# A gated two-block decoder on one core: quantisation groups padded by their minimum, inputs loaded in halves, work redistributed among the engines

## Time and profile before

| what | value |
|---|---|
| median of 3 runs | 260.58 us (259.67 to 260.72) |
| the profiled execution | 258.16 us, its span 256.4 us |
| busy shares | PE 86%, DVE 64%, ACT 53%, POOL 44% |
| mean granted clock of TensorE | 0.960 |

### The profile page before, as it was taken

The page is one execution under the profiler, slowest core; times in us unless marked ns, Lnnn a source line. Parts: engine busy times, 40 slices in busy tenths (PEclk is TensorE's granted clock), DMA queues, the critical chain, the costliest instruction groups (busy, mean ns, idle before and its releaser), DMA issues. The chain is left out here.

```text
span 256.4 us, 5210 instructions
## 1 busy us (share of the span) xinstructions
PE 221.2 (86%) x1960; PEld 179.7 (70%) x1960; DVE 165.0 (64%) x430; ACT 135.9 (53%) x286; POOL 111.6 (44%) x163
## 2 busy tenths in 40 slices
PE   8489988591999898985889999997998999999992
PEld 8366656470867676765767787776886788888882
DVE  1777886799289999885536667778746433353333
ACT  2144875974276786767876677764354222222230
POOL 3211111167166667656193777778947600000000
PEclk9869999978699999998999999999999999999999
DMA  4999001750000000000000000000000000020002
GB/s 138 382 359 364 21 1 18 309 165 0 3 0 1 0 3 0 1 0 4 0 3 3 3 3 4 3 3 3 4 1 0 0 3 0 0 84 0 0 0 82
DMA packets 9288, 12.59 MB, mean 49 GB/s; under 512 B 1072, under 2 KB 7984, under 8 KB 9264
## 3 DMA queue, kind: packets, MB, share of 16 engines
q1 hardware_dynamic: 8832, 12.07, 13.4%
q10 hardware_dynamic: 432, 0.20, 0.3%
HBM read 11.22 MB, written 1.05 MB: 48 GB/s over the span
## 5 line engine op out<-in xcount | busy, mean ns | idle before, releaser
L1416 PE MATMUL PB<-SGN,WHI 128*128 128x512 f32 x128 | 40.5, 398 | 0.0
L768 DVE TENSOR_TENSOR QM<-SIL,PB 128x512 f32<-128x512 f32 x16 | 11.0, 688 | 31.7 <-ACT SIL L1102 31.7
L1219 PE MATMUL PB<-SGN,XQH 128*128 128x512 f32 x64 | 27.3, 426 | 2.5 <-DVE XQL L619 2.5
L315 POOL TENSOR_TENSOR RSTD<-MVS,MHALF 128x1 f32<-128x1 f32 x24 | 14.5, 603 | 32.4 <-DVE MVS L473 32.4
L1102 ACT ACTIVATE SIL<-PB 128x512 f32<-128x512 f32 x16 | 9.6, 599 | 34.8 <-PE PB L1416 34.8
L1433 PE MATMUL PB<-WHI,SGN 128*128 128x256 f32 x128 | 25.8, 284 | 1.4 <-DVE SGN L776 1.4
L1219 PE MATMUL PB<-SGN,XQL 128*128 128x512 f32 x64 | 26.6, 415 | 0.0
L1416 PEld LDWEIGHTS PB<-SGN,WHI 128*128 128x128 f32 x128 | 23.1, 188 | 4.2
L1416 PE MATMUL PB<-SGN,WLO 128*128 128x512 f32 x64 | 25.2, 394 | 0.0
L356 POOL TENSOR_TENSOR HBQ<-HBQ,HSD 128x512 f32<-128x512 f32 x16 | 16.7, 1046 | 17.6 <-ACT HBQ L1008 17.6
L1058 ACT ACTIVATE HBQ<-PB 128x512 f32<-128x512 f32 x32 | 17.5, 614 | 10.8 <-PE PB L1356 10.8
(11 more groups left out here) (138 smaller groups left out, 553.9 us busy)
## 6 DMA issues: line engine op xcount, KB each, us to landing
WRAW<-w_dram SPq DMA_DIRECT2D x3, 1024.0 KB, 9.5
...
CTX<-ctx_dram SPq DMA_DIRECT2D x1, 1024.0 KB, 11.5
...
```

The source lines that it names most:

```text
L315: nc.gpsimd.tensor_tensor(RSTD[:, bass.ds(t, 1)], MVS[:, bass.ds(t, 1), 1], MHALF[:], ALU.pow).then_inc(rstd_ready, 1)
L768: nc.vector.tensor_tensor(GU[:, b, :], SG[:, b, :], PB[2 * b + 1][:], ALU.mult).then_inc(d_g, 1)
L1219: mm = nc.tensor.matmul(PB[2 * half + m][:], part[:, p, c, :], sgn(m, c, a, b), start=(c == 0 and k == 0), stop=(c == DC - 1 and k == 1))
L1416: mm = nc.tensor.matmul(PB[2 * b + m][:], wcol(w_part, m, c, j), act_part[:, c, g * TG:(g + 1) * TG], start=(c == 0 and i == 0), stop=(c = ...
```

## The change

Several edits are made together.

- **Padded groups.** XN (normalised x) and HB (h) get 65 columns per group of 64; the 65th holds 1e-5, written once by GpSimd. The maximum over 65 columns is then already max(|x|, 1e-5), and the instruction that formed the step (lines 584 and 657) goes. The factor 127 moves: for x into a small GpSimd product (`x_factor`), for h into the scale of ScalarE's first rounding instruction, and 1/127 into the weights' scales WSC.
- **x for the quantised layer.** ScalarE normalises it (`norm_x`) from an offset that GpSimd prepares (`x_offset`). For the first two tiles GpSimd takes over scaling and multiplying back. The rounding (`x_round`) reads XV as 5 rows of 64 out of 65 and writes 320 columns to XW. The tiles of the first attention are still normalised by VectorE.
- **Loads in halves.** x, CTXT and CTX are loaded as first halves, then second halves; the small vectors but one go behind the weights.
- **k and v.** The eight parts go to step numbers 1 to 7 (two in step 2), k through bank 4 to ScalarE, v through bank 5 to VectorE. VectorE sums |w1| and |w2| in eight slices of 512; ScalarE writes the signs of w3 in stage A too. The product that sums the scales moves from behind the first `gate_up` to the last step of stage A, and the setup of stage C's vectors (`prepare_c`) from ahead of VectorE's step 0 of stage B to its steps 3 to 5.
- **Order.** `down_scale` moves from the end of VectorE's step 1 up behind its first product. ScalarE rounds the second half of the previous tile before its other work. `xt_c` of the first tile moves into the last step of stage B, `q` behind it, and ScalarE loads the exponential's table ahead of the last rounding.

The core of the diff:

```diff
 WARMUPS = 14
-KV_PARTS = (("k", 0), ("k", 1), ("v", 0), ("k", 2), ("v", 1), ("k", 3), ("v", 2), ("v", 3))
-KV_AT = (1, 2, 3, 4, 5, 6, 7, 8)
+KV_PARTS = (("k", 0), ("v", 0), ("k", 1), ("k", 2), ("v", 1), ("k", 3), ("v", 2), ("v", 3))
+KV_AT = (1, 2, 2, 3, 4, 5, 6, 7)
+SIGN_ORDER = (0, 2, 4, 6, 1, 3, 5, 7)
+SIGN_AT = {3: (0, 1, 2), 4: (3, 4), 5: (5, 6), 6: (7, 8), 7: (9, 10, 11)}
+ABS_AT = {3: (0, 1), 4: (2, 3), 5: (4,), 6: (5, 6), 7: (7,)}
...
+        XN = sb("XN", [P, 2, D // GS, GS + 1])
         XSD = sb("XSD", [P, 2, 4])
...
-        XV = sb("XV", [P, D])
+        XRS = sb("XRS", [P, 4])
+        XV = sb("XV", [P, D // GS + 1, GS + 1])
+        XW = sb("XW", [P, D + GS])
...
+        HB = sb("HB", [P, 2, FF // GS, GS + 1])
...
+            for half, names in enumerate((("x", "ctxt", "ctx"), ("x2", "ctxt2", "ctx2"))):
+                ts = slice(half * NT // 2, (half + 1) * NT // 2)
+                ns = slice(half * NT // 2 * P, (half + 1) * NT // 2 * P)
...
-                             ).then_inc(ld[part], 16)
-            sp.dma_start(CTXT[:], ctx_t.rearrange("c p n -> p c n")).then_inc(ld["ctxt"], 16)
-            sp.dma_start(CTX[:], ctx.rearrange("t p d -> p t d")).then_inc(ld["ctx"], 16)
+                             ).then_inc(ld[names[0]], 16)
+                sp.dma_start(CTXT[:, :, ns], ctx_t.rearrange("c p n -> p c n")[:, :, ns]
+                             ).then_inc(ld[names[1]], 16)
+                sp.dma_start(CTX[:, ts, :], ctx.rearrange("t p d -> p t d")[:, ts, :]
...
+            sp.dma_start(BK[:], bk).then_inc(ld["bk"], 16)
...
+            def x_offset(t):
+
+                nc.gpsimd.tensor_tensor(NMB[:, t:t + 1], MVS[:, t, 0:1], NEG1[:], ALU.mult
+                                        ).then_inc(nm_x, 1)
+                pool.wait_ge(nm_x, 2 * t + 1)
+                pool.wait_ge(rstd_ready, t + 3)
+                nc.gpsimd.tensor_tensor(NMB[:, t:t + 1], NMB[:, t:t + 1], RSTD[:, t:t + 1],
+                                        ALU.mult).then_inc(nm_x, 1)
...
+            def x_factor(t):
+                pool.wait_ge(b_xd, 5 * t + 2)
+                nc.gpsimd.tensor_tensor(XRS[:], XR[:], C127[:].broadcast_to([P, D // GS]),
+                                        ALU.mult).then_inc(b_xd, 1)
+
+            def x_scale(t, p):
+                x_factor(t)
+                pool.wait_ge(b_xd, 5 * t + 3)
+                nc.gpsimd.tensor_tensor(XV[:, 0:D // GS, 0:GS], XN[:, p, :, 0:GS],
+                                        XRS[:].unsqueeze(2).broadcast_to(x_groups), ALU.mult
+                                        ).then_inc(b_xd, 1)
+
+            def x_quantised(t, p):
+                pool.wait_ge(b_xd, 5 * t + 5)
+                pool.wait_ge(xt_done, NT + t - 1)
+                nc.gpsimd.tensor_tensor(x_view(XQ[:, p, :]), x_view(XW[:, 0:D]),
+                                        XSD[:, p, :].unsqueeze(2).broadcast_to(x_groups),
+                                        ALU.mult).then_inc(b_xq, 1)
+
+            def step_a(t, p):
+                if t in (6, 7):
+                    x_quantised(t - 6, t - 6)
+                if t in (5, 6):
+                    x_scale(t - 5, t - 5)
+                if live(t - 2):
+                    rstd(t - 2, t - 2)
+                    x_offset(t - 2)
...
-                if half == 0:
-                    norm(0, 0, 0)
-                    norm(1, 1, 0)
-                    dve.wait_ge(ld["mask"], 16)
-                    nc.vector.tensor_scalar(MASKB, MASK8[:], -1.0, NEG, ALU.add, ALU.mult
-                                            ).then_inc(set_dve, 1)
-
...
+            stats_half(0)
+            dve.wait_ge(ld["mask"], 16)
+            nc.vector.tensor_scalar(MASKB, MASK8[:], -1.0, NEG, ALU.add, ALU.mult
+                                    ).then_inc(set_dve, 1)
+            norm(0, 0, 0)
+            norm(1, 1, 0)
...
-                    valid_gate()
+                    stats_half(1)
+                    gate_rows()
...
-                for k in {3: (0, 1), 4: (2, 3), 5: (4, 5), 6: (6,), 7: (7,)}.get(t, ()):
-                    nc.vector.tensor_reduce(ABSP[:, k:k + 1], WRAW[:, 0, k * D:(k + 1) * D],
+                if t == 5:
+                    dve.wait_ge(ld["w0b"], 16)
+                for k in ABS_AT.get(t, ()):
+                    nc.vector.tensor_reduce(ABSP[:, k:k + 1], flat(WRAW)[:, k * 512:(k + 1) * 512],
                                             AX.X, ALU.add, apply_absolute_value=True
                                             ).then_inc(w_abs1, 1)
-
...
+                if t in (5, 6):
+                    x_round(t - 5)
+                if t in (4, 5):
+                    x_absmax(t - 4, t - 4)
+                    x_recip(t - 4)
+                if t == NT - 1:
+                    dve.wait_ge(w_abs1, NT)
+                    nc.vector.tensor_reduce(ABSS[:, 0:2],
+                                            ABSP[:, 0:NT].rearrange("p (m k) -> p m k", m=2), AX.X,
+                                            ALU.add).then_inc(wsum, 1)
+                    lo_x(0, 0)
+                    dve.wait_ge(wsum, 2)
+                    nc.vector.tensor_scalar(WSC[:, 0:2], PB[2][:, 0:2], 1.0 / (D * FF * QB), None,
+                                            ALU.mult).then_inc(wsc, 1)
+
...
+                dve.wait_ge(xn_done, t + 1)
                 need(dve, b_xq, t - 1)
-                nc.vector.tensor_reduce(XSD[:, p, :], x_view(XH[:, p, :]), AX.X, ALU.max,
+                nc.vector.tensor_reduce(XSD[:, p, :], XN[:, p, :, :], AX.X, ALU.max,
                                         apply_absolute_value=True).then_inc(b_xd, 1)
 
-            def x_step(t, p):
+            def x_recip(t):
                 dve.wait_ge(b_xd, 5 * t + 1)
-                nc.vector.tensor_scalar(XSD[:, p, :], XSD[:, p, :], Q_EPS, 1.0 / QB, ALU.max,
-                                        ALU.mult).then_inc(b_xd, 1)
...
-                    norm(u, p, 1)
                     x_absmax(u, p)
-                    x_step(u, p)
-                    x_recip(u, p)
+                    x_recip(u)
                 h_product(t, p, 0)
+                if t == 1:
+                    down_scale()
+                h_absmax(t, p, 0)
+                h_recip(t, p, 0)
                 if live(t - 1):
                     lo_h(t - 1, 0)
-                h_absmax(t, p, 0)
-                h_step(t, p, 0)
-                h_recip(t, p, 0)
                 if live(t - 2):
                     update_b(t - 2, p)
                 if live(t + 1):
                     lo_x(t + 1, 1 - p)
                 if live(u):
-                    x_round(u, p)
+                    x_round(u)
...
-                h_step(t, p, 1)
                 h_recip(t, p, 1)
                 if live(t - 1):
                     lo_h(t - 1, 1)
...
-                if t == 1:
-                    down_scale()
-
...
+            def norm_x(t, p):
+
+                act.wait_ge(nm_x, 2 * t + 2)
+                need(act, b_xd, 5 * (t - 2) + 4)
+                nc.scalar.activation(XN[:, p, :, 0:GS],
+                                     X[:, t, :].rearrange("p (g s) -> p g s", s=GS), ACT.Identity,
+                                     bias=NMB[:, t:t + 1], scale=RSTD[:, t:t + 1]
+                                     ).then_inc(xn_done, 1)
...
+                if t == 6:
+                    act.wait_ge(ld["w3"], 16)
+                if 3 <= t <= 5:
+                    norm_x(t - 3, (t - 3) % 2)
+                for k in SIGN_AT.get(t, ()):
+                    sign_slice(k)
...
+                nc.scalar.activation(h, h, ACT.Copy, bias=MAGIC, scale=QB).then_inc(b_w, 1)
...
+                if live(t - 1):
+                    round_h(t - 1, 1 - p, 1)
                     hi_h(t - 1, 0)
                 if live(t + 1):
                     hi_x(t + 1, 1 - p)
-                if live(t - 1):
-                    round_h(t - 1, 1 - p, 1)
+                else:
+                    copy_ht(0, 0, 4, xt_done, c_q, c_ht, 2 * NT)
                 silu(t, 1)
...
+                if live(t + 3):
+                    norm_x(t + 3, 1 - p)
+                if 2 <= t <= 6:
                     hi_slice(t - 2)
-
-            warm(ACT.Silu)
-            sign_w3(0)
-            act.wait_ge(ld["bias"], 16 * 8)
-            act.wait_ge(a_mk, NT)
-            act.wait_ge(wsc, 1)
-            pipeline(step_b, lag=0)
-            copy_ht(0, 0, 4, xt_done, c_q, c_ht, 2 * NT)
-            round_h(NT - 1, 1, 1)
-            hi_h(NT - 1, 0)
-            q_out(0)
-            hi_h(NT - 1, 1)
-
...
+            warm(ACT.Silu)
+            act.wait_ge(a_mk, NT)
+            act.wait_ge(wsc, 1)
+            pipeline(step_b, lag=0)
+            q_out(0)
             warm(ACT.Exp)
-            copy_ht(1, 1, 4, xt_done, c_q, c_ht, 2 * NT)
+            round_h(NT - 1, 1, 1)
+            hi_h(NT - 1, 0)
             for b in range(4):
                 exp_c(0, 0, b)
+            hi_h(NT - 1, 1)
```

(19 more changed lines are left out.)

438 lines of the change are left out of this document (199 added, 239 removed).

## The result

The changed kernel takes 243.63 us (median of 4 runs, 242.29 to 245.47), the kernel before beside it 260.65 (259.67 to 261.41): a ratio of 0.935, 95% interval 0.928 to 0.942. The forecast was 244.7, 239.5 to 251.

The account below looks back on a forecast made before the run. TensorE nearly fills stage A's loop; VectorE, held by GpSimd, lengthens stage B's steady steps; TensorE waits at B's start and end. Terms -2.0 - 7.1 - 4.8 - 2.0 = -15.9 give 242.3 profiled, 244.7 beside the median; range 239.5 to 251.

Parts of the forecast that it names:

- (a): Begin and stage A, up to the first gate_up: halved loads start the loop earlier; -2.0 us, between -3.4 and 0.
- rival 3: Stage A: VectorE bounds it, sums and evictions bunching in the middle steps; 2.0 us back, 246.7; chance 0.06.
- TensorE's 27.30 are unchanged: Loop of stage A: TensorE's busy time stays 27.30 us, so the loop itself has little to give.
- (b): First two steps of stage B, 21.74 us: they shrink to the later steps' length; -7.1 us, bounds -7.7 and -3.4.
- Rival 2: Start of stage B: the low clock remains, a new wait replacing the removed one; 3.7 us back, 248.4; chance 0.09.
- (c): Five steady steps of stage B, 41.31 us: VectorE no longer bounds; -4.8 us, bounds -6.1 and 0.
- my 7.3: Steady steps of stage B: forecast 7.3 us per step, TensorE's work at full clock, 7.55 x 0.97.
- longer than VectorE's 7.09: Steady steps of stage B before: 8.26 us each, longer than VectorE's busy 7.09, taken as 35.43 / 5.
- Rival 1: Steady steps of stage B stay at 8.26 us, GpSimd's queue full; 4.8 us back, 249.5; chance 0.13.
- (d): End of stage B, 19.19 us: wait of 3.31 goes, less the table load's 1.28; -2.0 us, bounds -3.3 and 0.
- The rest: Stages C and D, to the last product: they keep their instructions; 0 us change.
- Rival 4: All of stage B at the low clock from small recurring waits; slower, 25 us above the forecast, 269.5; chance 0.06.

Follow-up runs that it names:

- a_combined: Changed kernel with stage C's setup behind VectorE's step 7, ScalarE's exponentials last at stage B's end, and 24 instead of 14 products of ones: 242.62 us.
- a_whole_loads: Changed kernel with x loaded in its two halves first, then CTXT and CTX whole, as before: 245.38 us.
- b_scale_early: Kernel before, with only the instruction for the scale of w3 moved up behind the first product of VectorE's step 1: 257.11 us, ratio 0.989.
- a_setup_late: Changed kernel with five of eight setup instructions of stage C moved from VectorE's steps 3 to 5 of stage B to behind step 7: 243.62 us.
- a_load_late: Changed kernel with ScalarE's load of the exponential's table behind the last rounding instead of ahead of it: 246.43 us.
- a_tail: Changed kernel with ScalarE's list at the end of stage B reordered, the four exponentials of tile 0 last: 244.32 us.

## Why the prediction was right, point by point

**(a) Right in the mechanism, half the size.** From x to the loop's first scores it is 8.13 us before (13.87 - 5.74) and about 6.2 after (both tiles' scores stand in one row, begun at 10.60), 1.9 sooner, where I had 2.1. Then 1.3 of it went again, so that 0.64 are left; the other 0.31 of the 0.95 are x, which landed sooner. It did not go to VectorE as rival 3 had it (26.50 busy of 32.54; I had 26.5) but to the half clock, which in the kernel before ended at 17.16 and now at 19.11, and of which the loop, starting sooner, meets more. The step that failed is "TensorE's 27.30 are unchanged". From the second tile's scores on, where the loop of the earlier trace rows starts too, after and then a_combined have:

```profile
11.61:43.14 31.53, 29.35 (x117) 19.84 (x117) 26.41 (x98) 19.27 (x51) 9.33 (x25) 0.88 0.50 172
```

```profile
11.83:42.01 30.18, 26.26 (x118) 17.74 (x117) 26.31 (x98) 19.16 (x51) 9.33 (x25) 1.00 0.50 173
```

TensorE's work is 29.35 at a clock of 0.88, and 26.26 at 1.00. Which of halves and other edits of stage A gave what is left stays open: a_whole_loads is within the spread.

GpSimd's power took 1.32 beside the mask in its new place, against 1.03: 0.29 of the 0.69 us that I had as the limit. The Trainium skill, "SBUF — State Buffer", section "Who interferes with whom", by which the one that issues first holds the shared ports and the other blocks, had led me to weigh this. The row that I had called in agreement shows less than that: there the power of 1.50 us had started 0.18 us ahead of VectorE's instruction, so it shows no order.

**(b) Right, 1 us too small and outside its bound of -7.7.** Both steps together take 13.63, less than two of 7.04: the first is 5.11 long, since it has no tile before it to finish, which two equal steps left out. The main cause, the place of one instruction, is shown twice; what gave the last 3 us is not. Rival 2 did not come: the clock is 1.00.

**(c) The sum was exact, its working was not.** TensorE bounds the undisturbed steps at 6.93 and 7.00, under my 7.3, which I had taken for 7.55 at full clock; but b_scale_early, at 1.00 in these steps, has 7.50, so it was not the clock that made 7.55. GpSimd's 28.03 / 5 = 5.61 and ScalarE's 6.04 are what I took (5.6 and 6.1). But VectorE has 6.88 per step, not 5.4, and my 7.09 for before was too low to begin with. It is a mean with a first step of 4.48, part of whose work VectorE had done ahead while TensorE waited for WSC. The third and fourth step of before alone, columns as in the earlier trace rows, are

```profile
82.41:90.91 8.50, 7.51 (x45) 5.77 (x44) 8.29 (x21) 5.84 (x12) 5.86 (x8) 1.00 0.00 0
90.91:99.47 8.56, 7.53 (x44) 5.79 (x43) 8.35 (x21) 5.89 (x12) 5.91 (x8) 1.00 0.01 2
```

with VectorE, held by GpSimd as I had it, full but for 0.21 us: it bounds the step by itself, and "longer than VectorE's 7.09" holds of the mean alone. Then I took off five normalisations and ten small instructions, while the earlier trace rows has three and nine in the stretch, and I gave the setup of stage C no price where it was moved to. The setup makes two of the five steps VectorE's, and costs 0.88 by a_setup_late. The two errors, 7.3 too long and the setup left out, cancelled: that -4.8 came out was luck. Rival 1 was wrong in its engine: GpSimd never sets the step, while VectorE is idle for 0.1 to 0.2 us in two of them.

**(d) Right in sign, 1.2 too much.** I read the wait of 3.31 for XH as the stretch's price, less the table load. ScalarE's list was the bound behind it; a_load_late shows that the load's place doesn't matter, a_tail that the place of the exponentials does. Some 0.5 of the missing 1.2 is the fall of the clock at the end of B, which I had not counted: 18.41 to 18.63 in the four runs with ScalarE's list as it was and a fall there, 17.91 to 18.04 in the five without.

**The rest** was 0 by forecast, and 0.4 is measured, of the size that stage C and D differ by in runs without a fall there (126.48 to 127.02). Rival 4 did not come: stage B runs at 1.00 until 107.9, near its end.
